# Attention with heads, before its first batch: ScalarE converts queries ahead of keys and copies all strips, key work moved among the strips, safety bound earlier, flag turned round

## The chip, the cores and the metric

One core of a Trainium2 chip. The metric is the device time of one execution in microseconds (us), the median of several runs; lower is better. Engine names are those of the profile: PE (TensorE matmul), PEld (its weight loads), DVE (VectorE), ACT (ScalarE), POOL (GpSimd), SP (the queue that issues most transfers). PEq, PEldq and DVEq rows are of an engine's sequencer.

## The reference, cut to what matters

Four layers of cross attention and a feed-forward part run over x of shape 16 x 100 x 128, with a context of 16 x 1444 x 128. Layers 1, 2 and 3 have 16 heads of 8; the change is in their attention alone:

```python
qh, kh, vh = (proj(q, wq, bq), proj(k, wk, bk), proj(v, wv, bv))
scores = jnp.einsum('bhqd,bhkd->bhqk', qh, kh) / np.sqrt(DK).astype(jnp.float32)
attn = jax.nn.softmax(scores, axis=-1)
out = jnp.einsum('bhqk,bhkd->bhqd', attn, vh)
```

Layer 2 masks keys (`jnp.where(mask == 0, -1e9, scores)`), and layer 3 puts an RMS norm on queries and keys.

## The kernel before, in words

`heads_attention` runs three times (layer 1, 2, 3), each between a small `layernorm` and a feed-forward part; each stage ends in a barrier of all engines. Keys and values of all three layers were made in layer 0 and lie in HBM. Inside `layernorm` SP issues the loads of the first batch: weights, the two halves of the keys (`kraw`, semaphores `k_in[0]` and `k_in[1]`, each half 64 rows of the keys, laid on the partitions twice) and two batches of values.

Then comes a preparation that is done once a layer, and only behind it the 16 batches. Products run in a rounded type (float32r), so queries and keys are each split in a high part (the rounded value) and a low part (what rounding left):

- PE projects the queries in four groups of 400 columns (L795); DVE adds the bias (L993; L985 masked; L989 and L990 normed, followed by L998). In layer 2 one more small matmul (L804) counts valid keys, and DVE needs its result before L985. In layer 3 PE averages squares per head (L800) and ACT takes logarithm and exponential (L938, L939).
- ACT makes the high keys of batch 0 (L930, twice, one for each half), waits for the columns' loads, loads its function table (L942; L934 in layer 3), makes the high queries (L945, four); DVE makes the low ones (L1003, four).
- The *strips*: 16 pairs of matmuls (L815 with the high queries, L816 with the low ones) stack the queries into `qrep` through six PSUM banks. The even strips are copied out by ACT (L951), the odd ones by DVE (L1014), so strip n waits for the copy of strip n - 6 on its engine.
- DVE takes the largest query per column (L1005) and multiplies with the largest key (L1010, `prod`). PE, behind the last strip, makes a bias matmul (L818) and 16 small matmuls (L821) from `prod`; DVE reduces them to a bound (L1017 to L1020) and writes `unsafe`, a flag in memory.
- DVE makes the low keys of batch 0 (L1031, twice), with the block queries of batch 0 (L1040, `qstack`) between them. When L1031 has read a half of `kraw`, SP loads that half of the next batch.
- PE and DVE load the flag (L920, L1121) and branch (L921, L1122). `batches(True)` subtracts a row maximum and is long; `batches(False)` is short and is the one that these inputs take. The long one stands first in both engines' programs, the short one behind it.

In `batches`, PE makes three score matmuls a slot (L873; 16 slots a batch), ACT takes the exponential of a slot (L960), and PE multiplies with the values (L835). PE's first L873 waits for both L1031 of the batch (`k_low`) and for L1040 (`qstack_ready`). DVE prepares the keys and queries of the next batch meanwhile. The last DVE work of a layer is a normalisation and an addition into x; the barrier is behind it.

Of the kernel before, what the change touches and what calls it, by code (L numbers as in the profile page):

```python
# [13 lines left out]
I32 = mybir.dt.int32  # L14
# [10 lines left out]
H, HD = 16, 8  # L25
# [20 lines left out]
KCHUNKS = [(0, 512), (512, 512), (1024, SK - 1024)]  # L46
SAFE = 60.0


# [616 lines left out]
def heads_attention(nc, k, ins, layer, store):  # L666
# [3 lines left out]
    with Scope(nc, f"a{layer}") as c:  # L670
# [66 lines left out]
        bound = c.sb("bound", [1, 2])  # L737
        unsafe = c.sb("unsafe", [1, 1], I32)
        rowmax = c.sb("rowmax", [SQ, H])
# [20 lines left out]
        q_full, q_free, q_ready, q_squared, q_high, q_low = c.sems("q_full q_free q_ready q_squared q_high q_low")  # L760
        stacked, rep_act, rep_dve, k_high, k_low = c.sems("stacked rep_act rep_dve k_high k_low")
        dropped, biased = c.sems("dropped biased")
# [29 lines left out]
        def _(pe):  # L792
            pe.wait_ge(w_in, 32)
            for g in range(TG):
                pe.matmul(score[:, g * 512:g * 512 + NTG], wq[:, :], k.xnT[:, g * NTG:(g + 1) * NTG],  # L795
                          start=True, stop=True).then_inc(q_full, 1)
            if normed:
                for g in range(TG):
                    pe.wait_ge(q_squared, g + 1)
                    pe.matmul(score[:, g * 512:g * 512 + NTG], k.blockavg[:, :],  # L800
                              qsq[:, g * NTG:(g + 1) * NTG], start=True, stop=True).then_inc(q_full, 1)
            if masked:
                pe.wait_ge(counted, 1)
                pe.matmul(numer[:, 0:B], k.ones[:, :], anyrow[:, :], start=True, stop=True).then_inc(counted, 1)  # L804
            pe.wait_ge(stack_made, 2)
            for n in range(TG * GROUPS):
                at, g = divmod(n, GROUPS)
                if g == 0:
                    pe.wait_ge(q_ready, TG)
                    pe.wait_ge(q_high, at + 1)  # L810
                    pe.wait_ge(q_low, at + 1)
                if n >= 6:
                    pe.wait_ge((rep_act, rep_dve)[n % 2], (n - 6) // 2 + 1)
                to = score[:, (n % 6) * 512:(n % 6) * 512 + NTG]
                pe.matmul(to, stack[:, 0, g, :], qhigh[:, at * NTG:(at + 1) * NTG], start=True, stop=False)  # L815
                pe.matmul(to, stack[:, 1, g, :], qlow[:, at * NTG:(at + 1) * NTG], start=False, stop=True).then_inc(stacked, 1)  # L816
            pe.wait_ge(prod_ready, 1)
            pe.matmul(misc[0:SQ, 0:D], bvrep[:, :], wo[:, :], start=True, stop=True).then_inc(bias_full, 1)  # L818
            pe.wait_ge(prod_ready, 2)
            for b in range(B):  # L820
                last = pe.matmul(numer[0:1, b * H:(b + 1) * H], prod[:, b:b + 1], k.headmask[:, :], start=True, stop=True)  # L821
            last.then_inc(bound_full, 1)

# [56 lines left out]

            def batches(shifted):
                if masked and shifted:
                    pe.wait_ge(dropped, 1)
# [30 lines left out]

            pe.wait_ge(rep_act, TG * GROUPS // 2)
            pe.wait_ge(rep_dve, TG * GROUPS // 2)
            pe.wait_ge(cleared, 3)
            pe.wait_ge(flag_ready, 1)
            pe.sem_inc(parted, 1)
            flag = pe.value_load(unsafe[0:1, 0:1], min_val=0, max_val=1)  # L920
            with pe.If(flag):  # L921
                batches(True)
            with pe.Else():
                batches(False)

        @block.scalar
        def _(act):
            for half in range(2):
                act.wait_ge(k_in[half], 64)
                act.copy(kstack[:, 0, half * KHALF:(half + 1) * KHALF], kraw[:, half, :]).then_inc(k_high, 1)  # L930
            act.wait_ge(cols_in, COLS)
            if normed:
# [14 lines left out]
            act.wait_ge(q_high, TG)  # L947
            for n in range(0, TG * GROUPS, 2):
                at, g = divmod(n, GROUPS)
                act.wait_ge(stacked, n + 1)  # L950
                act.copy(qrep[:, g, at * BG:(at + 1) * BG, :],  # L951
                         score[:, (n % 6) * 512:(n % 6) * 512 + NTG].rearrange("p (b q) -> p b q", q=SQ)).then_inc(rep_act, 1)
# [12 lines left out]
        def _(dve):  # L965
# [39 lines left out]
            steps.done(dve.tensor_reduce(qmax[:, :], qT[:, :, :], X, ALU.max, apply_absolute_value=True))  # L1005
            dve.tensor_copy(bvrep[:, :], cols[:, 1:2].to_broadcast([128, SQ])).then_inc(prod_ready, 1)
            if normed:
                dve.tensor_scalar(prod[:, :], qmax[:, :], HD ** 0.5, None, ALU.mult).then_inc(prod_ready, 1)
            else:
                dve.tensor_tensor(prod[:, :], qmax[:, :], store.peak[:, layer - 1, :], ALU.mult).then_inc(prod_ready, 1)  # L1010
            for n in range(1, TG * GROUPS, 2):
                at, g = divmod(n, GROUPS)
                dve.wait_ge(stacked, n + 1)
                dve.tensor_copy(qrep[:, g, at * BG:(at + 1) * BG, :],  # L1014
                                score[:, (n % 6) * 512:(n % 6) * 512 + NTG].rearrange("p (b q) -> p b q", q=SQ)).then_inc(rep_dve, 1)
            dve.wait_ge(bound_full, 1)
            steps.done(dve.tensor_reduce(bound[:, 0:1], numer[0:1, 0:B * H], X, ALU.max))  # L1017
            steps.done(dve.tensor_scalar(bound[:, 1:2], bound[:, 0:1], SAFE / HSCALE, -1.0, ALU.is_lt, ALU.mult))
            dve.memset(numer[:, :], 0.0).then_inc(numer_free, 1)
            dve.tensor_scalar(unsafe[:, :], bound[:, 1:2], 1.0, None, ALU.add).then_inc(flag_ready, 1)  # L1020

# [11 lines left out]
            def block_queries(b):  # L1033
                j = b % 2
                if b == 0:
                    dve.wait_ge(rep_act, TG * GROUPS // 2)
                    dve.wait_ge(rep_dve, TG * GROUPS // 2)
                if b >= 2:
                    dve.wait_ge(scored, (b - 1) * SLOTS)
                dve.tensor_tensor(qstack[:, j, :, :].rearrange("p (g j) q -> p g j q", j=GH),  # L1040
                                  qrep[:, :, b, :].unsqueeze(2).to_broadcast([128, GROUPS, GH, SQ]),
                                  k.groupmask[:, :].unsqueeze(1).unsqueeze(3).to_broadcast([128, GROUPS, GH, SQ]),
                                  ALU.mult).then_inc(qstack_ready, 1)
# [67 lines left out]

            for half in range(2):
                low_keys(0, half)
                if half == 0:
                    block_queries(0)
            if masked:
# [3 lines left out]
            dve.sem_inc(parted, 1)  # L1120
            flag = dve.value_load(unsafe[0:1, 0:1], min_val=0, max_val=1)  # L1121
            with dve.If(flag):  # L1122
                batches(True)
            with dve.Else():
                batches(False)

# [1135 lines left out]
```

## Time and profile before

| | us |
|---|---|
| median of 3 runs | 2391.35 (2389.32 to 2392.45) |
| the profiled execution | 2404.29 |
| its span, first to last instruction | 2402.5 |
| PE busy | 2112.4 (88%) |
| ACT busy | 1443.8 (60%) |
| DVE busy | 1321.0 (55%) |
| mean granted TensorE clock | 0.93 of full speed |

The profiled execution is one run with the profiler on. Spans and starts below are its own. A row of the timeline gives start, length, engine, line, operation, output and input, how many were merged, and in brackets how long the engine had been idle and what ended it.

### The profile page before, as it was taken

The page shows a single profiled execution, that of the slowest core. Times are in us where ns is not written, and L with a number is a line of the kernel's source. Part 1 is how long each engine was busy: PE and PEld are TensorE (multiplying, and loading weights), DVE is VectorE, ACT ScalarE, POOL GpSimd, SP SyncE. Part 2 cuts the span into 40 slices and gives each one's busy share as a digit, 9 for nine tenths or more (in the row PEclk, how much of TensorE's full clock was granted, in tenths as well). Part 3 has the DMA queues.
Part 4 walks back from the last instruction along what each step waited for, and adds up shares of the span by engine and source line. Part 5 has one row for each costly group of instructions (what it writes and reads, how often), then busy time and mean ns, then how long its engine had stood idle before and what let it go on. Part 6 is the DMA issues. An engine that isn't in the chain of part 4 may idle for free. (4 is left out here: it accounts for less than half of the span.)

```text
span 2402.5 us, 42615 instructions
## 1 busy us (share of the span) xinstructions
PE 2112.4 (88%) x16862; PEld 1384.1 (58%) x16862; DVE 1321.0 (55%) x1823; ACT 1443.8 (60%) x1784; POOL 235.0 (10%) x305
## 2 busy tenths in 40 slices
PE   5877978979889669999956999997985999997999
PEld 3554855847648346666634666664654666664554
DVE  4653343334343566777557788864456777753333
ACT  2335455445554458888835888885425888885431
POOL 1005033141330400000010000001010000000000
PEclk9988989989989879999967999998987999998999
DMA  5859346255462467777416777742026777742000
GB/s 193 261 173 342 120 145 256 105 205 187 149 249 98 153 158 182 185 185 185 109 41 161 181 184 185 185 108 64 1 43 141 183 185 185 185 117 71 0 8 7
DMA packets 119757, 352.82 MB, mean 147 GB/s; under 512 B 20160, under 2 KB 54846, under 8 KB 118942
## 3 DMA queue, kind: packets, MB, share of 16 engines
q1 hardware_dynamic: 105774, 322.41, 49.2%
q0 software_dynamic: 13776, 27.54, 3.7%
q8 instruction: 144, 2.36, 0.4%
q14 instruction: 63, 0.52, 0.1%
HBM read 257.58 MB, written 91.23 MB: 145 GB/s over the span
## 5 line engine op out<-in xcount | busy, mean ns | idle before, releaser
L960 ACT ACTIVATE a_probs<-a_score 128x1200 f32<-128x1200 f32 x768 | 857.9, 1169 | 177.0 <-PE a_score L873 177.0
L873 PE MATMUL a_score<-a_qstack,a_kstack 128*128 128x400 f32 x2304 | 552.4, 372 | 29.9 <-DVE a_kstack L1031 28.9
L873 PEld LDWEIGHTS a_score<-a_qstack,a_kstack 128*128 128x128 f32 x2304 | 379.5, 190 | 200.2 <-issue 121.6
L835 PE MATMUL a_numer<-a_probs,a_v 128*18 128x200 f32 (+1 forms) x9216 | 471.5, 335 | 0.0
L835 PEld LDWEIGHTS a_numer<-a_probs,a_v 128*18 128x18 f32 (+1 forms) x9216 | 228.6, 97 | 184.4 <-issue 88.4
L1031 DVE TENSOR_TENSOR a_kstack<-a_kraw,a_kstack 64x2888 fp32r<-64x2888 f32 x96 | 303.8, 3164 | 3.1
L1026 DVE CAST a_kstack<-a_kraw 128x2888 fp32r<-128x2888 f32 x90 | 149.8, 1665 | 14.8 <-DVE a_own L1088 8.8
L1040 DVE TENSOR_TENSOR a_qstack<-a_qrep,k_groupmask 128x1600 fp32r<-128x1600 f32 x48 | 87.6, 1826 | 119.6 <-PE a_score L873 119.1
L1684 PEld LDWEIGHTS f0r_ph<-f0r_xsT,f0r_w 128*128 128x128 f32 x896 | 118.7, 198 | 30.6 <-issue 12.5
L1684 PE MATMUL f0r_ph<-f0r_xsT,f0r_w 128*128 128x128 f32 x896 | 122.6, 281 | 9.3 <-DVE f0r_xsT L1872 9.3
L2084 ACT ACTIVATE f_hidden<-f_ph,f_b 128x400 f32<-128x400 f32 x128 | 75.9, 594 | 88.3 <-PE f_ph L2008 80.8
L1695 PE MATMUL f0r_py<-f_w,f0r_hidden 128*128 x896 | 119.6, 277 | 4.6 <-DVE f0r_xs L1843 2.7
L2150 DVE TENSOR_TENSOR f_hidden<-f_hidden,f_pw 128x1600 f32<-128x1600 f32 x32 | 58.1, 1820 | 112.5 <-PE f_pw L2025 112.5
L1773 ACT ACTIVATE f0r_hidden<-f0r_ph 128x512 f32<-128x512 f32 x112 | 66.9, 597 | 84.8 <-PE f0r_ph L1684 84.8
L1695 PEld LDWEIGHTS f0r_py<-f_w,f0r_hidden 128*128 128x128 f32 x896 | 109.0, 192 | 6.9 <-issue 6.9
L1087 DVE TENSOR_SCALAR a_own<-a_numer,k_first 128x200 f32<-128x200 f32 x48 | 20.4, 426 | 150.3 <-PE a_numer L835 150.3
L637 DVE SCALAR_TENSOR_TENSOR kv_made<-f0r_ph,kv_cols,kv_kinv 128x512 f32<-128x512 f32 x32 | 23.9, 750 | 141.7 <-ACT kv_kinv L600 131.2
L1843 DVE COPY f0r_xs<-f0r_py 128x128 f32<-128x128 f32 x112 | 32.6, 291 | 124.6 <-PE f0r_py L1695 124.6
L530 ACT COPY kv_vst<-f0r_pr 128x384 f32<-128x384 f32 x96 | 46.1, 481 | 89.5 <-PE f0r_pr L521 89.5
L2034 PE MATMUL f_py<-f_hidden,f_w 128*128 128x400 f32 x256 | 94.0, 511 | 0.0
L2008 PE MATMUL f_ph<-k_xnT,f_w 128*128 128x400 f32 x256 | 92.3, 507 | 0.0
L1837 DVE COPY f0r_w<-f_w 128x512 f32 x112 | 51.9, 463 | 68.7 <-issue 48.5
(360 smaller groups left out, 2728.1 us busy)
## 6 DMA issues: line engine op xcount, KB each, us to landing
a_kraw<-keys SPq DMA_DIRECT2D x384, 361.0 KB, 6.2
values<-kv_vst SPq DMA_DIRECT2D x32, 1296.0 KB
a_v<-values SPq DMA_DIRECT2D x48, 864.0 KB, 5.8
keys<-kv_made SPq DMA_DIRECT2D x48, 722.0 KB
l0a_ctxT<-in_ctxT SPq DMA_DIRECT2D x16, 722.0 KB, 7.0
kv_ctxT<-in_ctxT SPq DMA_DIRECT2D x16, 722.0 KB, 6.3
l0a_ctx<-in_ctx SPq DMA_DIRECT2D x16, 704.0 KB
l0a_mask<-in_mask_BxSxS_ik SPq DMA_DIRECT2D x16, 564.1 KB
```

The costliest lines, as they stand in the source:

```text
L835: last = pe.matmul(numer[32 * g:32 * g + PC, p * 2 * SQ:(p + 1) * 2 * SQ], v[0:rows(t), j, t, (2 * g + p) * PC:(2 * g + p + 1) * PC], prob ...
L873: last = pe.matmul(to, kstack[:, j, g * SK + t * 128:g * SK + (t + 1) * 128], qstack[:, j, g * GH:(g + 1) * GH, :], start=True, stop=not s ...
L960: act.activation(probs[:, n % NP, :].rearrange("p (g q) -> p g q", g=SPAN), slot_ps[:, n % 2, :, 0:GQ], ACT.Exp, scale=HSCALE).then_inc(ex ...
L1026: dve.tensor_copy(kstack[:, b % 2, half * KHALF:(half + 1) * KHALF], kraw[:, half, :]).then_inc(k_high, 1)
L1031: dve.tensor_tensor(low, kraw[64:128, half, :], low.bitcast(F32), ALU.subtract).then_inc(k_low, 1)
L1040: dve.tensor_tensor(qstack[:, j, :, :].rearrange("p (g j) q -> p g j q", j=GH), qrep[:, :, b, :].unsqueeze(2).to_broadcast([128, GROUPS, G ...
L1684: last = pe.matmul(ph[:, j, ci * 128:(ci + 1) * 128], w1[:, j, ci * 128:(ci + 1) * 128], xsT[:, s // GB % 2, s % GB, :], start=True, stop= ...
L1695: last = pe.matmul(py[:, j, 0:D], hidden[:, j, ci, :], m.w2[:, bass.ds(ex, 1), ci, :], start=(ci == 0), stop=(ci == FC - 1))
L1773: act.activation(hidden[:, n % 2, :, :], ph[:, n % 2, :].rearrange("p (c q) -> p c q", q=128), ACT.Silu).then_inc(silued, 1)
L2008: pe.matmul(ph[:, m % 3, 0:NTG], w1[:, e, ci * 128:(ci + 1) * 128], k.xnT[:, g * NTG:(g + 1) * NTG], start=True, stop=True).then_inc(up_fu ...
L2034: pe.matmul(py[:, g % 2, 0:NTG], w2[:, e, ci, :], hidden[:, g % 2, e, ci, :], start=(e == 0 and ci == 0), stop=False)
L2084: act.activation(hidden[:, g % 2, e, ci, :], ph[:, m % 3, 0:NTG], ACT.Gelu, bias=b1[:, e, ci:ci + 1]).then_inc(gelued, 1)
```

## The change

1. ACT's two high key copies no longer stand first. `high_keys(0)` stands behind the high queries (and after the wait for all low queries), `high_keys(1)` between the eighth and the ninth strip copy. The wait for `cols_in` on ACT goes.
2. ACT copies all 16 strips; DVE none. Strip n waits for `rep_act` n - 5.
3. The 16 bound matmuls stand behind strip 9 (`BOUND_AT`); `prod` is made before `bvrep`.
4. DVE: `low_keys(0, 0)`, then the bound and the flag (one instruction less), then `block_queries(0)`, then `low_keys(0, 1)`. Block queries wait for the four strips of their own group of batches only.
5. Layer 2: the count matmul stands behind the first of four projections.
6. The flag is `safe`, and `batches(False)` is the branch that falls through; PE's wait for the last strip copies is inside `batches`.

```diff
             for g in range(TG):
                 pe.matmul(score[:, g * 512:g * 512 + NTG], wq[:, :], k.xnT[:, g * NTG:(g + 1) * NTG],
                           start=True, stop=True).then_inc(q_full, 1)
+                if masked and g == 0:
+                    pe.wait_ge(counted, 1)
+                    pe.matmul(numer[:, 0:B], k.ones[:, :], anyrow[:, :], start=True, stop=True).then_inc(counted, 1)
...
                 if n >= 6:
-                    pe.wait_ge((rep_act, rep_dve)[n % 2], (n - 6) // 2 + 1)
+                    pe.wait_ge(rep_act, n - 5)
...
-            pe.wait_ge(prod_ready, 1)
+                if n == BOUND_AT:
+                    pe.wait_ge(prod_ready, 1)
+                    for b in range(B):
+                        last = pe.matmul(numer[0:1, b * H:(b + 1) * H], prod[:, b:b + 1], k.headmask[:, :], start=True, stop=True)
+                    last.then_inc(bound_full, 1)
+            pe.wait_ge(prod_ready, 2)
             pe.matmul(misc[0:SQ, 0:D], bvrep[:, :], wo[:, :], start=True, stop=True).then_inc(bias_full, 1)
...
-            flag = pe.value_load(unsafe[0:1, 0:1], min_val=0, max_val=1)
+            flag = pe.value_load(safe[0:1, 0:1], min_val=0, max_val=1)
             with pe.If(flag):
+                batches(False)
+            with pe.Else():
                 batches(True)
-            with pe.Else():
-                batches(False)
...
-            for half in range(2):
+            def high_keys(half):
                 act.wait_ge(k_in[half], 64)
                 act.copy(kstack[:, 0, half * KHALF:(half + 1) * KHALF], kraw[:, half, :]).then_inc(k_high, 1)
-            act.wait_ge(cols_in, COLS)
...
-            for n in range(0, TG * GROUPS, 2):
+            high_keys(0)
+            for n in range(TG * GROUPS):
                 at, g = divmod(n, GROUPS)
+                if n == TG * GROUPS // 2:
+                    high_keys(1)
                 act.wait_ge(stacked, n + 1)
...
-            for half in range(2):
-                low_keys(0, half)
-                if half == 0:
-                    block_queries(0)
+            low_keys(0, 0)
+            dve.wait_ge(bound_full, 1)
+            steps.done(dve.tensor_reduce(bound[:, 0:1], numer[0:1, 0:B * H], X, ALU.max))
+            dve.tensor_scalar(safe[:, :], bound[:, 0:1], SAFE / HSCALE, None, ALU.is_lt).then_inc(flag_ready, 1)
+            dve.memset(numer[:, :], 0.0).then_inc(numer_free, 1)
+            block_queries(0)
+            low_keys(0, 1)
```

ACT's program in layer 1, from the start of the preparation to the exponentials, before:

```order
L930 CAST a_kstack<-a_kraw 128x2888 x2
L942 ACT_TABLE_LOAD
L945 CAST a_qhigh<-a_probs 128x400 x4
L951 CAST a_qrep<-a_score 128x400 x8
L960 ACTIVATE a_probs<-a_score 128x1200 x256
```

and with the change (lines moved by a few):

```order
L943 ACT_TABLE_LOAD
L946 CAST a_qhigh<-a_probs 128x400 x4
L931 CAST a_kstack<-a_kraw 128x2888
L955 CAST a_qrep<-a_score 128x400 x8
L931 CAST a_kstack<-a_kraw 128x2888
L955 CAST a_qrep<-a_score 128x400 x8
L964 ACTIVATE a_probs<-a_score 128x1200 x256
```

The table load and the high queries now stand ahead of both key copies, and the strip copies are 16 instead of 8, with the second key copy in their middle.

DVE's program in layer 1, from the low queries to the second low keys, before:

```order
L1003 TENSOR_TENSOR a_qlow<-a_probs,a_qhigh 128x400 x4
L1005 TENSOR_REDUCE a_qmax<-a_probs 128x16
L1006 COPY a_bvrep<-a_cols 128x100
L1010 TENSOR_TENSOR a_prod<-a_qmax,k_peak 128x16
L1014 CAST a_qrep<-a_score 128x400 x8
L1017 TENSOR_REDUCE a_bound<-a_numer 1x1
L1018 TENSOR_SCALAR a_bound<-a_bound 1x1
L1019 MEMSET a_numer 128x512
L1020 TENSOR_SCALAR a_unsafe<-a_bound 1x1
L1031 TENSOR_TENSOR a_kstack<-a_kraw,a_kstack 64x2888
L1040 TENSOR_TENSOR a_qstack<-a_qrep,k_groupmask 128x1600
L1031 TENSOR_TENSOR a_kstack<-a_kraw,a_kstack 64x2888
```

and the same stretch with the change:

```order
L1007 TENSOR_TENSOR a_qlow<-a_probs,a_qhigh 128x400 x4
L1009 TENSOR_REDUCE a_qmax<-a_probs 128x16
L1013 TENSOR_TENSOR a_prod<-a_qmax,k_peak 128x16
L1014 COPY a_bvrep<-a_cols 128x100
L1025 TENSOR_TENSOR a_kstack<-a_kraw,a_kstack 64x2888
L1107 TENSOR_REDUCE a_bound<-a_numer 1x1
L1108 TENSOR_SCALAR a_safe<-a_bound 1x1
L1109 MEMSET a_numer 128x512
L1033 TENSOR_TENSOR a_qstack<-a_qrep,k_groupmask 128x1600
L1025 TENSOR_TENSOR a_kstack<-a_kraw,a_kstack 64x2888
```

Before, eight strip copies and the four instructions of the bound stood between `prod` and the first low keys; now the bound stands between the two halves of the low keys.

PE's program at the end of layer 1's `batches(False)`, with the change:

```order
L907 MATMUL a_misc<-a_wo,a_att 100x128 x2
L922 UNCONDITIONAL_BRANCH
L857 MATMUL a_score<-a_kstack,a_qstack 100x512 x2
```

L857 is the first instruction of `batches(True)`, which now stands behind the short body: the jump at its end passes over the long one. Before, L904 (the same matmul) was followed by the end of the stage.

## Rows read from the trace of the kernel before

**Rows 1.** Waits: who waited for whom; us in total, times, longest us.

```profile
PE a_score L873 <- DVE a_kstack L1031: 28.9, 3, 9.6
```

**Rows 2.** Timeline of layer 1, from the preparation to the first slots.

```profile
839.08 1.99 DVE L993 TENSOR_SCALAR a_probs<-a_score,a_cols 128x400 f32<-128x400 f32 x3 [0.62 <-PE a_score L795]
841.64 2.60 ACT L930 CAST a_kstack<-a_kraw 128x2888 fp32r<-128x2888 f32 x1 [7.08 <-DMA a_kraw<-keys]
849.04 2.60 ACT L930 CAST a_kstack<-a_kraw 128x2888 fp32r<-128x2888 f32 x1 [4.81 <-DMA a_kraw<-keys]
...
853.51 2.03 DVE L1003 TENSOR_TENSOR a_qlow<-a_probs,a_qhigh 128x400 fp32r<-128x400 f32 x4 [12.44 <-ACT a_qhigh L945]
...
862.81 0.95 PE L821 MATMUL a_numer<-k_headmask,a_prod 128*1 128x16 f32 x32
863.80 0.41 DVE L1017 TENSOR_REDUCE a_bound<-a_numer 1x1 f32<-1x256 f32 x1 [0.53 <-PE a_numer L821]
...
864.57 0.48 DVE L1019 MEMSET a_numer<- 128x512 f32 x1 [0.18 <-DVE a_bound L1018]
...
868.33 1.82 DVE L1040 TENSOR_TENSOR a_qstack<-a_qrep,k_groupmask 128x1600 fp32r<-128x1600 f32 x1
870.18 3.16 DVE L1031 TENSOR_TENSOR a_kstack<-a_kraw,a_kstack 64x2888 fp32r<-64x2888 f32 x1
...
873.40 2.37 PE L873 MATMUL a_score<-a_qstack,a_kstack 128*128 128x400 f32 x6 [9.64 <-DVE a_kstack L1031]
...
874.87 2.23 ACT L960 ACTIVATE a_probs<-a_score 128x1200 f32<-128x1200 f32 x2 [12.05 <-PE a_score L873]
...
883.20 1.17 ACT L960 ACTIVATE a_probs<-a_score 128x1200 f32<-128x1200 f32 x1 [0.20 <-PE a_score L873]
```

**Rows 3.** Timeline of layer 2, the same stretch.

```profile
1262.23 0.29 PE L804 MATMUL a_numer<-a_anyrow,k_ones 128*128 128x16 f32 x2
...
1263.37 2.26 DVE L985 SCALAR_TENSOR_TENSOR a_probs<-a_score,a_cols,a_anyvalid 128x400 f32<-128x400 f32 x4
...
1293.69 2.37 PE L873 MATMUL a_score<-a_qstack,a_kstack 128*128 128x400 f32 x6 [9.64 <-DVE a_kstack L1031]
```

**Rows 4.** Timeline of layer 3, the same stretch.

```profile
1799.22 3.24 PE L800 MATMUL a_score<-a_probs,k_blockavg 128*128 128x400 f32 x8
...
1812.91 0.59 ACT L938 ACTIVATE a_qlog<-a_score,a_eps 128x400 f32<-128x400 f32 x1
...
1818.26 2.03 DVE L1003 TENSOR_TENSOR a_qlow<-a_probs,a_qhigh 128x400 fp32r<-128x400 f32 x4
...
1837.15 2.37 PE L873 MATMUL a_score<-a_qstack,a_kstack 128*128 128x400 f32 x6 [9.64 <-DVE a_kstack L1031]
```

**Rows 5.** The tile qrep: ns min/median/max of a copy, first and last start.

```profile
L951 ACT CAST a_qrep<-a_score x24: 492/493/494, 855.6 to 1826.1; 128x400 fp32r<-128x400 f32 x24
```

**Rows 6.** The two branches on the flag, same columns.

```profile
L921 PEldq COMPARE_BRANCH  x3: 3397/3816/3976, 866.1 to 1829.8; - x3
...
L1122 DVEq COMPARE_BRANCH  x3: 73/73/77, 865.8 to 1829.6; - x3
```

**Rows 7.** The drains that close layer 1's and then layer 3's attention, same columns.

```profile
L91 PEldq DRAIN  x1: 1218/1218/1218, 1212.7 to 1212.7; - x1
L91 DVEq DRAIN  x1: 17/17/17, 1215.0 to 1215.0; - x1
...
L91 PEldq DRAIN  x1: 725/725/725, 2175.9 to 2175.9; - x1
L91 DVEq DRAIN  x1: 17/17/17, 2177.7 to 2177.7; - x1
```

**Rows 8.** Windows in layer 1: busy (instructions) by engine, granted clock, DMA share, GB/s.

```profile
880.00:882.00 2.00, 2.00 (x26) 1.53 (x30) 1.97 (x2) 1.23 (x2) 0.00 (x0) 1.00 1.04 220
```

**Rows 9.** Timeline of layer 2, exponentials at their steady pace.

```profile
1303.28 2.24 ACT L960 ACTIVATE a_probs<-a_score 128x1200 f32<-128x1200 f32 x2 [0.20 <-PE a_score L873]
...
1308.31 2.23 ACT L960 ACTIVATE a_probs<-a_score 128x1200 f32<-128x1200 f32 x2 [0.20 <-PE a_score L873]
```

More of the change, by code:

```diff
@@ L47 @@
 SAFE = 60.0
+BOUND_AT = 9
 def rows(t):
@@ L737, in heads_attention @@
         bound = c.sb("bound", [1, 2])
-        unsafe = c.sb("unsafe", [1, 1], I32)
+        safe = c.sb("safe", [1, 1], I32)
         rowmax = c.sb("rowmax", [SQ, H])
@@ L760, in heads_attention @@
         q_full, q_free, q_ready, q_squared, q_high, q_low = c.sems("q_full q_free q_ready q_squared q_high q_low")
-        stacked, rep_act, rep_dve, k_high, k_low = c.sems("stacked rep_act rep_dve k_high k_low")
+        stacked, rep_act, k_high, k_low = c.sems("stacked rep_act k_high k_low")
         dropped, biased = c.sems("dropped biased")
@@ L801, in _ @@
                               qsq[:, g * NTG:(g + 1) * NTG], start=True, stop=True).then_inc(q_full, 1)
-            if masked:
-                pe.wait_ge(counted, 1)
-                pe.matmul(numer[:, 0:B], k.ones[:, :], anyrow[:, :], start=True, stop=True).then_inc(counted, 1)
             pe.wait_ge(stack_made, 2)
@@ L816, in _ @@
                 pe.matmul(to, stack[:, 1, g, :], qlow[:, at * NTG:(at + 1) * NTG], start=False, stop=True).then_inc(stacked, 1)
-            pe.wait_ge(prod_ready, 1)
+                if n == BOUND_AT:
[4 more added lines that the diff above has]
+            pe.wait_ge(prod_ready, 2)
             pe.matmul(misc[0:SQ, 0:D], bvrep[:, :], wo[:, :], start=True, stop=True).then_inc(bias_full, 1)
[L819 to L822, printed above, removed]
             def mix(b, t, p):
@@ L881, in batches @@
             def batches(shifted):
+                pe.wait_ge(rep_act, TG * GROUPS)
                 if masked and shifted:
@@ L913, in batches @@
                                 mix(b, x // PAIRS, x % PAIRS)
-            pe.wait_ge(rep_act, TG * GROUPS // 2)
-            pe.wait_ge(rep_dve, TG * GROUPS // 2)
             pe.wait_ge(cleared, 3)
@@ L1005, in _ @@
             steps.done(dve.tensor_reduce(qmax[:, :], qT[:, :, :], X, ALU.max, apply_absolute_value=True))
-            dve.tensor_copy(bvrep[:, :], cols[:, 1:2].to_broadcast([128, SQ])).then_inc(prod_ready, 1)
             if normed:
@@ L1010, in _ @@
                 dve.tensor_tensor(prod[:, :], qmax[:, :], store.peak[:, layer - 1, :], ALU.mult).then_inc(prod_ready, 1)
[L1011 to L1020, printed above, removed]
+            dve.tensor_copy(bvrep[:, :], cols[:, 1:2].to_broadcast([128, SQ])).then_inc(prod_ready, 1)
             def high_keys(b, half):
@@ L1034, in block_queries @@
                 j = b % 2
-                if b == 0:
-                    dve.wait_ge(rep_act, TG * GROUPS // 2)
-                    dve.wait_ge(rep_dve, TG * GROUPS // 2)
+                if b % BG == 0:
+                    dve.wait_ge(rep_act, (b // BG + 1) * GROUPS)
                 if b >= 2:
@@ L1120, in _ @@
             dve.sem_inc(parted, 1)
-            flag = dve.value_load(unsafe[0:1, 0:1], min_val=0, max_val=1)
+            flag = dve.value_load(safe[0:1, 0:1], min_val=0, max_val=1)
             with dve.If(flag):
+                batches(False)
+            with dve.Else():
                 batches(True)
-            with dve.Else():
-                batches(False)
 def softmax_rows(dve, act_done, ch, logits, top, e, total, inv, probs, exp_ready, exped, E):
```

## The prediction

> **What bounds the stretch now.** I read the page first: PE is busy 88% of the span, so only stretches in which PE stands still are worth much to this change. Then the waits: PE's first score matmul of a layer waits 9.6 us for the low keys, three times, 28.9 us in all [rows 1]. Then the timeline around that wait, since a wait behind a chain says little about the chain's length. The reader is to see in [rows 2] a chain that runs through ACT in program order: ACT's first high key copy starts when its half of the keys has landed (841.64), the second when the second half has (849.04), and only behind it ACT makes the high queries, although DVE had all four groups of queries ready at 839.08 + 1.99 = 841.07. DVE's low queries start at 853.51, after 12.44 us idle. Behind them all is serial: strips, bound matmuls (862.81), the reduction (863.80), low keys, block queries (868.33), low keys (870.18), PE at 873.40. Layers 2 and 3 repeat it, with second halves landing at 1269.73 and 1809.00 and the same 9.64 us [rows 3, 4]. So PE does next to nothing from the projection to the first slot, 30 us and more a layer, and what is saved there is saved in the end: before the first slot everything waits for PE, and the slots then run one behind the other.
>
> The sum is made against the profiled execution, 2404.29 us (span 2402.5). It is 12.9 us above the median of the three runs, 2391.35, and I take the same difference off both.
>
> **The new chain, from T0, the end of the low queries.** ACT's order is now high queries, key copy (2.60), eight strip copies, key copy (2.60), eight strip copies. A strip copy lasts 0.49 [rows 5]. How close they follow each other is not shown; two exponentials of 1.17 take 2.23 together [rows 2], which is 0.11 less than their sum, so 0.38 to 0.49, and I take 0.43. ACT is done at T0 + 2.6 + 3.4 + 2.6 + 3.4 + hops of 0.2 = T0 + 12.2.
>
> DVE goes beside it. Its largest query, `prod` and `bvrep` fill the time of ACT's first key copy. Low keys (3.16) run from T0 + 2.65 to T0 + 5.8. The bound matmuls stand behind strip 9, which needs the fourth copy, T0 + 4.35; a strip of 0.4 (two matmuls; six of that width take 2.37 at the lower clock, 0.8 a pair, and half of it at the full clock) and the bound's 0.95 give T0 + 5.7, about the same moment. Reduction, comparison and memset take about 1.05 (863.80 to the memset's end at 865.05, less the one removed step), block queries 1.85, second low keys 3.2: T0 + 11.9. Both chains end within 0.3 us of each other, and PE starts at the later, T0 + 12.25. The table load goes ahead of the high queries into time in which ACT now stands idle (7.08 us before its first key copy [rows 2]); the dropped wait for the columns and the narrower wait of the block queries (the first four copies, done at T0 + 4.35) cost and give nothing. The eight DVE copies and one comparison that are taken away (0.57 a copy at most) are worth nothing by themselves; the eight copies added on ACT (3.4) are on the path, and are in the sum.
>
> - Layer 1: biases end at 841.07, low queries 2.03 later, T0 = 843.1 [rows 2]. PE starts at 855.35 instead of 873.40: **18.0**.
> - Layer 2: the count matmul goes from behind the last projection (1262.23) to behind the first. It delays the projections by some 0.7 (two matmuls at the lower clock), and its result no longer holds the first three biases up: the last bias ends at 1262.9 + 0.6 = 1263.5 instead of 1263.37 + 2.26 = 1265.6. T0 = 1265.55, PE at 1277.8 instead of 1293.69 [rows 3]: **15.9**.
> - Layer 3: from the first logarithm (1812.91) to the end of the low queries (1818.26 + 2.03) it takes 7.4. The logarithm needs only the first average of squares, which starts at 1799.22 and takes about 0.75. T0 = 1807.35, PE at 1819.6 instead of 1837.15 [rows 4]: **17.5**.
>
> Together 51.4. The keys are there in time: ACT asks for the second half at T0 + 6.05, that is 849.15, 1271.6 and 1813.4, and the halves landed at 849.04, 1269.73 and 1809.00. SP's loads of batch 1's keys follow the low keys, so the first goes out some 19 us earlier and stays as far ahead of PE as before or further; no value load stands behind them.
>
> **The turned flag.** Before, both engines jumped over the long body at the start. PE's branch there took 3.4, 3.8 and 4.0 us, DVE's 0.07 [rows 6]. It was hidden: PE began it at 866.1 and had to wait until 873.40 anyway. Now both fall through at the start and jump over the same body at the end of a layer. PE's sequencer comes to its end when the last matmul is under way, where its drain starts now, and the barrier waits for DVE, whose drain starts 2.3 us later (1212.7 and 1215.0; in layer 3 1.8 later, 2175.9 and 2177.7) [rows 7]; layer 2 repeats layer 3 (1632.9, 1634.7). A jump of 3.4 to 4.0 sticks out by 3.4 - 2.3 = 1.1, 4.0 - 1.8 = 2.2 and 3.8 - 1.8 = 2.0: **5.3 given back**. What it would be at the least is nothing, if PE reaches its jump sooner than its drain shows. Left as it was, the jump would stand behind the last strip, at about T0 + 11, and would end some 3 us behind PE's new start, so turning it still pays.
>
> The row shows a price of 3.4 to 4.0 for one engine and 0.07 for the other. The Trainium skill has two rules. "Advanced Engine Details and Errata", Control Flow Timing, gives about 51 ns for a branch and 108 ns for compare-and-branch; by that the change would give nothing back and come out 5.3 lower, and PE's rows disagree. "Runtime: NRT & Kernel Launch", Instruction fetch mechanics, says that a taken branch out of the two pages that are held must fetch its target first; PE's rows agree, and it speaks against the change.
>
> **PE's clock.** At 873.40 the first six score matmuls take 2.37 and the sequence from the first exponential to the seventh takes 8.33 (874.87 to 883.20) where four slots later take 5.03, so six take 7.55 [rows 2, 9]. The first slots run at the lower clock, since PE had stood still; at 880 to 882 the grant is 1.00 [rows 8]. With the change PE has strips until shortly before its first slot. If the clock is still at 2.4 GHz there, a layer gains 0.8 in these slots and about 0.5 in the first; if not, nothing. No row decides between 0 and 3.9; I take the middle, **2.0**.
>
> **Sum.** 51.4 - 5.3 + 2.0 = 48.1: 2404.29 becomes 2356.2, and the median 2391.35 becomes **2343.2**.
>
> **The rivals.**
> 1. *DVE's jump costs what PE's does.* DVE is the last engine of a layer, so all of it would be exposed: 3.4 + 4.0 + 3.8 = 11.2 in place of 5.3. Time 2349.1. For it: DVE had until 873.40 to fetch, and 0.07 may be the branch without what comes behind. Against it: PE's record includes its stall. By the rule of the Trainium skill on fetching it would be so, if the long body does not fit in what DVE holds.
> 2. *PE at 1.2 GHz through the strips.* Strips and bound matmuls then take twice as long, the strip 0.8 and the bound 1.9; PE falls a strip behind ACT, the bound comes 1.9 later and DVE's chain, 0.3 behind ACT's, becomes the bound: 1.6 a layer, and no gain in the first slots. 4.8 + 2.0 = 6.8, time 2350.0. For it: PE stands still for 2 us twice in the stretch.
> 3. *The reordering does not do what it says*, since the keys land later than now: instructions, table load and value loads share the queues. With 4 us of delay 3.9, 2.1 and 0 are lost, time 2349. Against it: nothing in the change adds a transfer ahead of them.
> 4. *Slower: the clock stays low.* In a batch PE is busy all 2.00 of 2 us at full clock [rows 8] and a slot takes 1.26. At half the clock 16 slots cost 20 us more. If the broken-up strips kept the grant away for 2.4 batches in all, the gain would be gone; a whole batch in each layer gives 2343 + 60 = 2403. Against it: the clock comes back within 7 us of dense slots each time.
>
> **Chances.** Forecast 0.63 (its own range 2336 to 2348: copies at 0.38 or 0.49 move 1 us a layer, the clock's term 2 either way, the jump from 0 to 5.3); rival 1 0.15, rival 2 0.13, rival 3 0.05, rival 4 0.02, and 0.02 for something that eats the gain without a name. The range 2336 to 2353 holds the forecast and rivals 1 to 3 in most of their width. A measurement tells 0.2% (4.8 us) from no change; only rival 4 and part of the unnamed rest are not faster: faster 0.96, within 0.2% 0.02, slower 0.02.
>
> **What would show it.** PE's first L873-matmul at 12.3 us behind the last low query in each layer, and ACT, not DVE, as what it waits for; ACT's copies 0.43 apart; the second key copy starting without a wait; PE's unconditional branch of 3.4 to 4.0 us at the end of each layer and the barrier 1 to 2 us behind DVE's drain; DVE's own below 0.1. The prediction is wrong if the key halves hold ACT up, if the stretch from T0 takes over 14 us, or if the layer's end grows by more than 2.5 us.

## The result and the profile after

The changed kernel takes **2352.85 us** (median of 4 runs, 2348.54 to 2356.95), the kernel before on the same chip 2391.9. The ratio is 0.9847, 95% interval 0.983 to 0.9863: faster by 1.53%, that is 36.6 us of 2391.35, where 48.1 were forecast. 2343.2 would have been a ratio of 0.9799.

In the profiled executions PE is busy 90% instead of 88%, ACT 62% instead of 60%, DVE 56% instead of 55%. The page's groups after:

```profile
L964 ACT ACTIVATE a_probs<-a_score 128x1200 f32<-128x1200 f32 x768 | 857.7, 1169 | 149.3 <-PE a_score L875 149.3
L875 PE MATMUL a_score<-a_qstack,a_kstack 128*128 128x400 f32 x2304 | 551.7, 372 | 9.8 <-DVE a_kstack L1025 7.7
```

PE's score matmuls waited 28.9 us for the low keys [rows 1], now 7.7.

The two spans, 2402.5 and 2355.2, differ by 47.3, more than the ratio says. 11.2 of it lies in layer 0, whose code is the same: layer 1's layernorm starts at 827.71 before, at 816.51 after. So I compare stages, not spans. Each row is a sum over layers 1 to 3, from starts and ends in the two timelines: the layernorm's first DVE instruction, the last low query's end (T0), the first score matmul, the last out-projection matmul (L904, now L907), the next stage's first DVE instruction.

| stage, us | before | after | difference | forecast |
|---|---|---|---|---|
| layernorm to T0 | 90.07 | 55.87 | -34.2 | |
| T0 to first score matmul | 52.18 | 37.64 | -14.5 | |
| both | 142.25 | 93.51 | -48.7 | -51.4 |
| batches, to the last out-projection | 1017.16 | 1017.64 | +0.5 | -2.0 |
| end of the layer | 8.98 | 20.52 | +11.5 | +5.3 |
| the rest of layers 1 to 3 | 406.40 | 407.02 | +0.6 | 0 |
| sum | | | -36.1 | -48.1 |

The stages' 36.1 agree with the ratio's 36.6. Three terms are off, all the same way: the end by 6.2, the preparation by 2.7, the first slots (the row of the batches) by 2.5; the stretches that the change does not touch add 0.6.

Timeline of layer 1 after, to be laid beside [rows 2]:

```profile
830.71 2.02 DVE L1007 TENSOR_TENSOR a_qlow<-a_probs,a_qhigh 128x400 fp32r<-128x400 f32 x4
832.77 2.60 ACT L931 CAST a_kstack<-a_kraw 128x2888 fp32r<-128x2888 f32 x1 [1.41 <-DVE a_qlow L1007]
835.28 3.25 ACT L955 CAST a_qrep<-a_score 128x400 fp32r<-128x400 f32 x8
835.40 3.16 DVE L1025 TENSOR_TENSOR a_kstack<-a_kraw,a_kstack 64x2888 fp32r<-64x2888 f32 x1 [0.61 <-ACT a_kstack L931]
838.29 1.01 PE L821 MATMUL a_numer<-k_headmask,a_prod 128*1 128x16 f32 x32
838.34 2.68 ACT L931 CAST a_kstack<-a_kraw 128x2888 fp32r<-128x2888 f32 x1
839.34 0.41 DVE L1107 TENSOR_REDUCE a_bound<-a_numer 1x1 f32<-1x256 f32 x1 [0.77 <-PE a_numer L821]
840.43 1.79 DVE L1033 TENSOR_TENSOR a_qstack<-a_qrep,k_groupmask 128x1600 fp32r<-128x1600 f32 x1
840.84 3.35 ACT L955 CAST a_qrep<-a_score 128x400 fp32r<-128x400 f32 x8
842.26 3.16 DVE L1025 TENSOR_TENSOR a_kstack<-a_kraw,a_kstack 64x2888 fp32r<-64x2888 f32 x1
845.52 1.33 PE L875 MATMUL a_score<-a_qstack,a_kstack 128*128 128x400 f32 x6 [2.82 <-DVE a_kstack L1025]
846.41 2.23 ACT L964 ACTIVATE a_probs<-a_score 128x1200 f32<-128x1200 f32 x2 [2.23 <-PE a_score L875]
849.04 2.23 ACT L964 ACTIVATE a_probs<-a_score 128x1200 f32<-128x1200 f32 x2 [0.40 <-PE a_score L875]
852.87 2.23 ACT L964 ACTIVATE a_probs<-a_score 128x1200 f32<-128x1200 f32 x2 [1.60 <-PE a_score L875]
855.73 2.23 ACT L964 ACTIVATE a_probs<-a_score 128x1200 f32<-128x1200 f32 x2 [0.62 <-PE a_score L875]
```

Neither key copy waits for a DMA. The first eight strip copies take 3.25, so they start 0.39 apart ((3.25 - 0.49) / 7), the second eight 3.35, and ACT is done at 844.19. DVE's chain ends at 845.42, 1.2 later, and starts PE. In it DVE stands still for 0.77 before the reduction, behind bound matmuls. The granted clock of the same stretch (columns as in [rows 8]):

```profile
836.00:838.00 2.00, 2.00 (x8) 1.56 (x7) 2.00 (x1) 2.00 (x7) 0.00 (x0) 0.64 1.00 385
838.00:840.00 2.00, 2.00 (x36) 1.65 (x35) 1.12 (x3) 2.00 (x3) 0.00 (x0) 0.50 1.07 376
844.00:846.00 2.00, 0.47 (x3) 0.51 (x4) 1.94 (x3) 0.19 (x1) 0.00 (x0) 1.00 1.03 220
846.00:848.00 2.00, 1.22 (x6) 0.89 (x5) 2.00 (x1) 1.59 (x2) 0.00 (x0) 0.70 1.03 218
850.00:852.00 2.00, 2.00 (x19) 1.04 (x19) 1.46 (x2) 1.27 (x2) 0.00 (x0) 0.50 1.01 217
```

PE reaches the bound at 1.2 GHz. The first six score matmuls do run at 2.4 GHz (1.33 us, before 2.37 [rows 2]), and then the grant falls under the slots: from the first exponential to the seventh it takes 9.32 (846.41 to 855.73), before 8.33.

The end of layer 1. A DRAIN here is an engine's arrival at a barrier; L92 is the first barrier of the two that close a stage (L91 in [rows 7]), L95 the second. First the branch rows of the whole run (of the six on PE, the three at the layers' starts fall through in 0.08 to 0.09, and the three jumps at the ends take 3.3, 3.4 and 3.8), then the drains in layer 1, DVE's instructions around them, and a window of the jump:

```profile
L922 PEldq COMPARE_BRANCH  x6: 79/1712/3772, 842.7 to 2123.5; - x6
```

```profile
L1118 DVEq COMPARE_BRANCH  x6: 41/58/66, 841.8 to 2125.8; - x6
```

```profile
L92 PEldq DRAIN  x2: 60/516/972, 1189.0 to 1197.8; - x2
L92 DVEq DRAIN  x2: 58/1568/3079, 1190.1 to 1194.7; - x2
```

```profile
L95 PEldq DRAIN  x1: 8/8/8, 1190.5 to 1190.5; - x1
L95 DVEq DRAIN  x1: 128/128/128, 1192.4 to 1192.4; - x1
```

```profile
1187.03 0.18 DVE L178 BATCH_NORM_AGGREGATE k_mv<-k_moment 100x2 f32<-100x6 f32 x1
1192.84 0.17 DVE L211 TENSOR_SCALAR ln1f_var<-k_mv 100x16 f32<-100x16 f32 x1 [5.62 <-PEq L95]
```

```profile
1187.00:1190.00 3.00, 0.00 (x0) 0.00 (x0) 0.18 (x1) 0.00 (x0) 0.00 (x0) 0.50 0.03 8
```

PE jumps at 1185.2 and is at the barrier at 1189.0. DVE's last instruction ends at 1187.21, its branch is on record with at most 66 ns, and yet it arrives only at 1190.1, 2.9 us later (before: 0.3). At the second barrier it is late once more, 1192.4 when PE came at 1190.5. So DVE pays for its jump too, and its branch record does not show it. In layers 2 and 3 it is 2.9 and 3.8 (L178 ends at 1596.79 and 2125.58, DVE's drain is at 1599.64 and 2129.36), without the second delay.

Not all of the 11.5 is the jump. DVE's way to the first barrier grew by 8.8 in the three layers and the second delay holds layer 1 up by 1.7. Another 1.0 is PE's clock: in layers 2 and 3 the last four matmuls now run at a grant of 0.50, where before it was 0.92 and 0.84 in that stretch, and take 0.5 longer each time. Layer 2, the kernel before and then the change:

```profile
1632.88 0.68 PE L904 MATMUL a_misc<-a_wo,a_att 128*100 128x128 f32 x4 [1.90 <-DVE a_att L1097]
```

```profile
1594.75 1.18 PE L907 MATMUL a_misc<-a_wo,a_att 128*100 128x128 f32 x4 [1.90 <-DVE a_att L1090]
```

The trace also keeps the packets that bring instructions (queues 8 and 14 of the page). One of 16 KiB on queue 8 starts 1.0 behind PE's jump at 1185.17, takes 1.28, and PE goes on 1.5 after it has landed. One of 8 KiB on queue 14 starts 1.0 behind DVE's jump at 1187.25, takes 0.42, and DVE is at the barrier 1.4 after it has landed. So DVE's stall is a fetch. The next packet on queue 14 (1190.71, 0.47 long) lands 1.25 before DVE reaches the second barrier.

### The profile page after: what moved, and what is told of

The parts are those of the page before. It is cut to its first block and busy times, and to the rows that moved or that the text cites. A ratio compares the mean times of both kernels' runs of the same rounds, so it can differ in the third digit from the quotient of the medians.

```text
span 2355.2 us, 42618 instructions
## 1 busy us (share of the span) xinstructions
PE 2115.2 (90%) x16862; PEld 1384.8 (59%) x16862; DVE 1307.6 (56%) x1796; ACT 1449.9 (62%) x1808; POOL 234.8 (10%) x305
## 3 DMA queue, kind: packets, MB, share of 16 engines
q8 instruction: 143, 2.34, 0.4%
```

## The experiments

The theory behind the first five: the end of a layer costs 11.5 more because both engines now jump over the long body there, and DVE's jump, not PE's, sets it. The rivals: PE's jump sets it and DVE waits for PE; or the price is of the branch as such, not of what lies between. "Preps", "batches" and "ends" are the three sums of the table above.

**e1, the flag turned back, the rest of the change kept.**

```diff
             with pe.If(flag):
-                batches(False)
+                batches(True)
             with pe.Else():
-                batches(True)
+                batches(False)
```

The same on DVE, and `is_ge` for `is_lt` in the flag.

> The changed kernel with the flag turned back alone (the flag says unsafe, the long body stands first, both engines jump over it at the start). In the profile of the change the stretch from the last PE work of a layer to the first DVE work of the next stage grew from 3.3, 2.8 and 2.8 us to 7.7, 6.0 and 6.9. Theory A (both engines' jumps over the long body wait for instructions, DVE's too, although its branch row says 0.05): these stretches go back to about 3, together -11.5; at the start PE's jump begins behind the last strip and ends some 1 us behind the low keys, DVE's ends about when its second low keys end, together +2 to +4; time 2344 to 2347. Rival B (the ends grew for another reason, as what the earlier start does to drains or loads): the ends stay at 20.5 together, time 2353 to 2358.

Measured: 2370.2 us, ratio to the kernel before on the same chip 0.9849 (0.9823 to 0.9875), no difference from the change's 0.9847. Ends are 8.80, 11.7 lower, as before the change and as expected. But preps are 106.24, 12.7 higher, where 2 to 4 were expected, and so the expected gain in time did not come. First the branch on PE, then the timeline, then a window:

```profile
L922 PEldq COMPARE_BRANCH  x3: 6546/6830/6994, 858.0 to 1798.1; - x3
```

```profile
857.77 3.17 DVE L1025 TENSOR_TENSOR a_kstack<-a_kraw,a_kstack 64x2888 fp32r<-64x2888 f32 x1
865.13 2.34 PE L875 MATMUL a_score<-a_qstack,a_kstack 128*128 128x400 f32 x6 [7.13 <-issue]
866.21 0.29 DVE L1070 TENSOR_TENSOR a_bo<-a_bo,a_misc 100x128 f32<-100x128 f32 x1 [5.27 <-issue]
```

```profile
860.00:866.00 6.00, 0.87 (x3) 0.89 (x4) 0.94 (x1) 0.00 (x0) 0.00 (x0) 0.64 1.03 215
```

The low keys are ready at 860.94, and PE starts at 865.13: it is fetching. Its jump takes 6.5 to 7.0, before 3.4 to 4.0 [rows 6]. DVE, whose branch is on record at 857.1, starts the first instruction behind it at 866.21, 9.1 us later, 5.27 of it idle; in layers 2 and 3 it is 8.5 and 6.7 later. The DMA engines are full (share 1.01 to 1.03 in the three jumps); during the jumps at the layers' ends the share was 0.02 to 0.04. PE's instruction packet now starts 4.15, 3.46 and 4.08 behind the branch instead of 1.0, and then takes 1.3 to 1.4; DVE's starts 6.8, 6.2 and 4.3 behind. A jump has no fixed price, then, and e8 tests why.

**e2, the flag turned in the kernel before, nothing else.** The reverse exchange, with `unsafe` computed as its opposite.

> The kernel before with nothing changed but the flag, turned round as in the change. Theory A: the three layer ends grow from 9.0 together to 20 to 21, nothing is gained at the start (the jump was hidden there): 2392 + 11.5 = 2403. Rival B: no change, 2392.

Measured: 1.0038 (1.002 to 1.0056), ends 17.13 instead of 8.98, +8.2; preps 141.09, near the 142.25 of before. Little is won at the start, where the jump was hidden, and the end is lost. The end rose by less than in the change (11.5) and than expected, to 5.6, 5.9 and 5.6: DVE is at the first barrier 2.8 to 3.0 behind its jump in all three layers, in the change 3.5 in the third, and it is not late at the second. The jump is the same, but it stands elsewhere in DVE's program. That this is the reason is not shown.

**e3, e4, e5: nothing to jump over, on both engines, on DVE alone, on PE alone.** The long body, which these inputs never enter, is replaced by one instruction; so these kernels leave out the attention with a row maximum.

```diff
             with dve.Else():
-                batches(True)
+                dve.sem_inc(parted, 1)
```

> The change with the long body, which these inputs never take, cut to one semaphore increment on PE and DVE (left out: the attention with a row maximum). Theory A (the price is the fetch of a far target): the ends go back to 9 together, PE's branch rows fall under 0.2 us, time 2341 to 2344. Rival C (a taken jump costs this however short it is): ends stay at 20.5, 2353.

> The same cut on DVE alone; PE keeps its far jump. Theory A: DVE's drain starts at once behind its last instruction, the barrier then waits for PE's jump (3.4 to 3.8 us from its last matmul's start): ends of about 6.6, 4.5 and 4.5, 15.6 together. Rival D (all of the longer end is PE's jump, as the prediction had it): ends as in the change, 20.5.

> The change with the long body cut to one semaphore increment on PE alone (left out: PE's part of the attention with a row maximum, never taken here); DVE keeps its far jump. Theory A: DVE is the last engine of a layer and pays its whole fetch, so the ends stay at about 20 us together (7.7, 6.0, 6.9), although PE's branch falls to 0.1. Rival D (PE's jump is the price): ends near 9.

| | ends | layer 1, 2, 3 |
|---|---|---|
| before | 8.98 | 3.32, 2.83, 2.83 |
| the change | 20.52 | 7.67, 5.96, 6.89 |
| e3, both short | 9.46 | 2.83, 3.31, 3.32 |
| e4, DVE short | 13.93 | 4.84, 4.48, 4.61 |
| e5, PE short | 20.85 | 7.72, 6.21, 6.92 |

e3 measured 0.9776 (0.974 to 0.9813), its preps as in the change (93.27). PE's branch there:

```profile
L922 PEldq COMPARE_BRANCH  x6: 71/122/188, 848.1 to 2120.6; - x6
```

The three jumps at the ends, to a near target, take 0.17 to 0.19 here, so the price is of the far target. e5 has PE's jump short and ends as long as with it: PE's jump costs nothing while DVE's is there. Within 2 us of an engine's branch at the ends a packet on queue 14 starts in e5 and none on queue 8, in e4 it is the other way round, and in e3 there is neither. So queue 8 is PE's and queue 14 DVE's. e4 has PE's jump alone: 13.93 - 8.98 = 4.95 above before, where the forecast had 5.3 for just that; 0.5 of it is again PE's last matmuls at the lower clock. Steps of 0.5 between the layers of one row, as in e3 and before, are that clock too. e4 and e5 ran once (2366.11 and 2365.94); their stages are compared, not their times.

**e6, the last batch's DVE work and out-projection behind the branch.** If DVE must fetch, it should do it while PE still computes. DVE's body handles the last batch no more; a new `tail()` behind the If does.

```diff
-                for b in range(B + 1):
+                for b in range(B):
...
+            tail()
```

PE's last out-projection (now L928) stands behind its If, too.

> The change with the last steps of a layer put behind the two bodies, once for both: on DVE everything of the last round (it stands still for 11.9 us there, so its jump is hidden), on PE the last two matmuls L907. Theory A: DVE's drain follows its last instruction at once, ends of about 3 each; PE's jump of 3.4 to 3.8 now lies between L901 and L907, which stood 2.5 apart, so 1.0 to 1.3 of it shows, three times: 11.5 - 3.5 = 8 us less than the change, ratio to before 0.981, about 2347. Rival E (the jump only moves and costs the same wherever it stands): as the change, 0.985.

Measured: 0.9821 (0.9791 to 0.9852), ends 9.51, 11.0 lower: DVE's stall is hidden. PE's is not quite:

```profile
1185.75 0.61 PE L901 MATMUL a_misc<-a_own,k_spread 128*128 128x200 f32 x2 [1.01 <-DVE a_own L1114]
1189.45 1.18 PE L928 MATMUL a_misc<-a_wo,a_att 128*100 128x128 f32 x4 [3.10 <-issue]
```

The two stand 3.70 apart, before 2.51 (1210.16 and 1212.67), since PE now fetches between them: 1.2 in layer 1, 1.0 and 0.8 in layers 2 and 3, 3.0 in all, which the batches' 1019.77 contain.

**e7, e6 with the bound behind strip 5.** To take away the 0.77 that DVE waits for the bound matmuls.

```diff
-BOUND_AT = 9
+BOUND_AT = 5
```

> The same, and the bound matmuls behind strip 5 instead of strip 9. In the change DVE waits 0.77 for them in layers 1 and 2, since the strips ran at the lower clock there, and DVE's chain ends last. Theory: the first score matmul comes 0.8 earlier in two layers, 0 to 0.1 in layer 3: 1.5 less than the run before, ratio 0.9805, about 2345. Rival: ACT's copies end last, no gain.

Measured: 0.9809 (0.9781 to 0.9837). T0 to the first score matmul is 12.04 to 12.06 in all layers, in the change 12.79, 12.80 and 12.05. Layer 1:

```profile
840.99 0.95 PE L821 MATMUL a_numer<-k_headmask,a_prod 128*1 128x16 f32 x32 [0.89 <-DVE a_prod L1018]
844.86 0.41 DVE L1126 TENSOR_REDUCE a_bound<-a_numer 1x1 f32<-1x256 f32 x1
851.04 2.34 PE L875 MATMUL a_score<-a_qstack,a_kstack 128*128 128x400 f32 x6 [2.07 <-DVE a_kstack L1030]
```

The bound is made 3.9 before DVE wants it, and DVE has no idle time left. What e7 gains on e6 as a whole lies within the intervals.

**e8, e1 with quiet DMA queues during the jump.** SP loads no keys of batch 1 until PE has made the scores of the first slot.

```diff
+                    if b == 1:
+                        sp.wait_ge(scored, 1)
                     load_keys(sp, b, half)
```

> The change with the flag turned back, and the loads of the second batch's keys held until the first slot is scored. With the flag turned back PE's jump took 6.5 to 7.0 us and DVE stood still until 9 us behind its branch, at a DMA share of about 1.0; at the ends of layers, with the DMA queues empty, jumps took 3.3 to 4.0. Theory F (a jump waits for its instructions behind the data in the DMA queues): PE's branch falls to 3.4 to 4.0 and the stretch from the last low query to the first scores from 17 to 13 or 13.5; the later loads may cost 1 to 2 us in the first batches. Rival G (the length depends on where the jump lands or on the engine, not on traffic): PE's branch stays at 6.5 to 7.0, the stretch at 17.

```profile
L924 PEldq COMPARE_BRANCH  x3: 3350/3354/3502, 855.5 to 1791.2; - x3
```

```profile
854.00:860.00 6.00, 2.27 (x9) 1.97 (x10) 5.90 (x4) 2.97 (x8) 0.00 (x0) 0.84 0.04 12
```

```profile
857.99 0.29 DVE L1072 TENSOR_TENSOR a_bo<-a_bo,a_misc 100x128 f32<-100x128 f32 x1
858.98 2.34 PE L877 MATMUL a_score<-a_qstack,a_kstack 128*128 128x400 f32 x6 [3.48 <-issue]
```

With the DMA share at 0.04 instead of 1.03 the same jump takes 3.4 to 3.5 on PE and is hidden on DVE: preps 95.60 instead of 106.24, and T0 to the first score 14.2, 13.6 and 13.4 instead of 17. PE's instruction packet starts 1.0 behind the branch again, where in e1 it was 3.5 to 4.15. Of the 3.1 to 3.6 that a jump of PE costs more in e1, 2.5 to 3.1 is this wait before the packet starts. Batch 1's keys come late for it (batches +5.4 on the change), so the version is no gain (2364.9, one run).

**e9, only the queries ahead of the keys, in the kernel before.** How much of the 48.7 is the order on ACT alone?

```diff
-            for half in range(2):
-                act.wait_ge(k_in[half], 64)
-                act.copy(kstack[:, 0, half * KHALF:(half + 1) * KHALF], kraw[:, half, :]).then_inc(k_high, 1)
...
             for g in range(TG):
...
+            for half in range(2):
+                act.wait_ge(k_in[half], 64)
+                act.copy(kstack[:, 0, half * KHALF:(half + 1) * KHALF], kraw[:, half, :]).then_inc(k_high, 1)
```

> The kernel before with one step of the change alone: ACT makes the high queries ahead of both key copies; strips, bound and flag as before. The gain of the change before the first slot (48.7 us in the profiles) has two parts, the earlier end of the low queries T0 (11.6, 11.0 and 11.6 a layer) and the shorter way from there to the first scores (17.9, 17.5 and 16.9 became 12.8, 12.8 and 12.1). Theory: T0 comes as early as in the change, but both key copies (5.2) now stand ahead of the even strip copies, so T0 to first scores grows to about 20.5; the three preparations are 25 shorter than before in all. Rival: the way from T0 stays 17.5, 34 shorter.

```profile
833.39 2.60 ACT L947 CAST a_kstack<-a_kraw 128x2888 fp32r<-128x2888 f32 x1 [2.11 <-DMA a_kraw<-keys]
835.89 1.27 ACT L951 CAST a_qrep<-a_score 128x400 fp32r<-128x400 f32 x3
836.43 0.70 PE L815 MATMUL a_score<-a_qhigh,a_stack 128*128 128x400 f32 x1 [6.68 <-ACT a_qrep L951]
```

Preps 127.59, 14.7 under before (2376.54, one run). T0 comes nearly as early as in the change (56.7 behind the layernorms' starts in all, there 55.9), but the key copies now stand ahead of the strip copies, PE waits 6.68 for a free bank, and T0 to the first score rises to 25.2, 23.0 and 22.7. Of what lies above the 20.5 expected, ACT's wait for the second half of the keys is 2.1 in layer 1, and the strips behind it run at the lower clock, 0.54 a matmul. Most of the gain comes only with the copies and the low keys placed among the strips.

**e11, the change with the odd strips copied by DVE again, ahead of its first low keys.**

```diff
+            for n in range(1, TG * GROUPS, 2):
+                at, g = divmod(n, GROUPS)
+                dve.wait_ge(stacked, n + 1)
+                dve.tensor_copy(qrep[:, g, at * BG:(at + 1) * BG, :], ...)
```

> The change with one step undone: the odd strips are copied by DVE again, ahead of its first low keys. Theory: DVE's eighth copy needs ACT's copies behind the second key copy, so the first low keys start at T0 + 8.9 instead of T0 + 2.7 and everything behind them follows: T0 to first scores about 18.3 instead of 12.8, 5.5 a layer. Rival: ACT's chain, the longer one by the prediction, gets 1.7 to 3.4 shorter and the first scores come earlier or stay.

```profile
831.77 3.16 DVE L1031 TENSOR_TENSOR a_kstack<-a_kraw,a_kstack 64x2888 fp32r<-64x2888 f32 x1
841.30 2.34 PE L875 MATMUL a_score<-a_qstack,a_kstack 128*128 128x400 f32 x6 [9.96 <-DVE a_kstack L1031]
```

T0 to the first score is 19.4, 19.4 and 18.8, preps 18.6 above the change (2361.67, one run). The ends are 16.65, 3.9 lower than in the change, without a second delay, as in e2. The first low keys start at 831.77, 7.3 after ACT's first key copy has ended (821.91 + 2.60), in the change at once. So the copies that were taken off DVE are worth 6.2 a layer: they stood on its chain.

**e10 and e12, the change again and e7 again, on one chip.** To place the best version beside the change.

> The changed kernel itself once more, beside the next one on the same chip. 0.985 of the kernel before, as measured first.

> The change with the tail behind both bodies and the bound behind strip 5, once more, beside the change on the same chip. By its profile (ends 9.9 instead of 20.5, preparations 91.5 instead of 93.5, 2.6 more in the batches' stretch from PE's later last matmuls) it should be 10 us, 0.4%, faster than the change: 0.981.

Measured on one chip: before 2390.58, the change 2352.64, ratio 0.9845 (0.9821 to 0.9868); e7's kernel **2341.77**, 0.9798 (0.9773 to 0.9823). It is 10.9 us below the change. By stages preps are 90.96 against 93.23 (-2.3), ends 9.84 against 20.73 (-10.9), batches 1019.74 against 1017.72 (+2.0), together -11.2.

## Why the prediction was wrong, and where it was right

**Right: the bound and the big term.** PE's stand before the first slot was what the change removes; 48.7 of 51.4 came. The keys' halves did not hold ACT up; the batches kept their length to 0.5 in 1017. PE's own jump was sized rightly in sum: the forecast had 5.3 sticking out, e4 shows 4.95, of which the jump is 4.5.

**Wrong, the step that failed: "3.4 to 4.0 for one engine and 0.07 for the other".** It took DVE's branch record for DVE's price. DVE needs 2.9, 2.9 and 3.8 from its last instruction to the barrier, where it needed 0.3, and is 1.9 late at the second barrier of layer 1. Since DVE is the last engine of a layer, all of it is exposed: the ends rose by 11.5 instead of 5.3, by 4.3, 3.1 and 4.1 a layer, which is over the 2.5 that the prediction gave as a sign of being wrong. That is rival 1, whose arguments "0.07 may be the branch without what comes behind" and "DVE had until 873.40 to fetch" were the true ones: in the kernel before, too, a packet on queue 14 starts 1.0 behind each of DVE's three branches. That its sum, 11.2, is nearly the measured one is partly luck: it took PE's price for DVE's, while the 11.5 are 8.8 of DVE's first stall, 1.7 of a second one and 1.0 of PE's clock, which it did not have. e5 shows that DVE alone sets the end, e3 that it is the far target. The Trainium skill, "Runtime: NRT & Kernel Launch", Instruction fetch mechanics, says that most engines hold two instruction pages, 512 instructions in all, and that a taken branch outside of them fetches its target. DVE's long body has some 525 to 550 instructions in the built program, and its stall agrees; with the body gone (e3) the stall is gone. No run has a body of a length between, so the 512 themselves are not shown. That rule stood in the prediction, with the body's length left uncounted.

**Off in size: the preparation, 2.7.** T0 came 1.9 later in all than forecast: it lies 16.2, 17.0 and 22.6 behind the layernorm's start, where the forecast's T0s lie 15.4, 17.3 and 21.3 behind it. The rest, 0.9, is the chain behind T0. I had ACT ending last, with copies 0.43 apart; at 0.39 it is done at T0 + 11.5. DVE ends last, 12.05 when nothing holds it up (e7), and in layers 1 and 2 it waited 0.77 for bound matmuls at 1.2 GHz. That is a part of rival 2, at half its price a layer.

**Off in sign: the first slots, 2.5.** The clock was up at the first slot, as I had hoped, and fell between 846 and 848. Over the batches 0.5 was lost where 2.0 was booked as a gain. Rows of before could not decide this; booking half of an unproven gain made the sum too low.

**Wrong beside the sum: "turning it still pays".** It was argued with the jump's price of the kernel before, 3.4 to 4.0, and by that the flag left as it was would have been 3 a layer behind. Its price there is nearly twice that under load, 6.5 to 7.0, and 12.7 in three layers, but the end gives 11.7 back: the turn is a wash in the changed kernel (0.9847 and 0.9849), and a loss of 0.38% by itself (e2). Only with its fetch hidden (e12) does the turn pay.

## What to carry to other kernels

A branch over a long body cost a fetch on both engines that took it here, whatever the branch record said: look at the gap to the next instruction or drain, and place the jump where that engine has slack, also at a stage's end. Where one engine ends a stage, move its last work behind the jump. And a chain of helpers is shortened by counting each engine's queue in order; a copy given from DVE to ACT paid here because the copies stood ahead of DVE's critical work.

## What the runs showed of the hardware that was not expected

- A far jump's price depends on the DMA traffic. PE: 3.3 to 4.0 at a DMA share of 0.02 to 0.24 (after's ends, e8, before), 6.5 to 7.0 at 1.01 to 1.03 (e1). DVE: 2.9 to 3.8 quiet, 6.7 to 9.1 at 1.02. e8 changes the traffic and brings PE back to 3.4. The instruction packets show where the time goes: with quiet queues they start 0.7 to 1.5 behind the branch and in e1 3.5 to 4.15 (PE) and 4.3 to 6.8 (DVE), while from the landing to the end of PE's jump it is 1.4 to 1.5 in e8 and 1.5 to 1.75 in e1. What holds the packet back for that time is not on record.
- PE's branch row contains its fetch stall, DVE's (41 to 77 ns) does not. The Trainium skill, "Advanced Engine Details and Errata", Control Flow Timing, gives some 51 ns for a branch and 108 for compare-and-branch; PE's branches in e3, 71 to 75 where they fall through and 169 to 188 where they jump near, are of that order, its far jumps are not.
- DVE was late a second time, at the next barrier, in layer 1 only (1192.4 against 1190.5), again in e5 and e10, and not in e2 and e11. A second instruction packet lands 1.25 before it arrives, as the first did 1.4 before the first barrier, so a second fetch is likely. No run tests it.
- PE's grant was 1.00 at the first slot of layer 1 (845.5), 0.70 in 846 to 848 and 0.50 in 850 to 852, though PE was at work. In e7, with the bound elsewhere, the first six score matmuls took 2.34, so the grant there had fallen already. No run isolates what makes the difference.
